# Edge words of 22 bits, lookups of the left-over maxima moved behind, and the short tile's neighbour sums with x as weights

## The reference, cut to what matters

```python
# layer 0: attention over neighbours
q = x[sub] @ Wq.T + bq ; k = x[obj] @ Wk.T + bk          # for the 10,000 pairs
scores = zeros(8, n, n).at[:, sub, obj].set((q * k).sum(-1) / 8)
scores = where(adj == 0, -inf, scores); diagonal = 1e-7
x = layernorm(x + (softmax(scores).sum(0) / 8) @ x)
# layer 1: graph convolution
x = layernorm(x + adj @ (x @ W) + bias)
```

## Time and profile before

| | |
|---|---|
| median of 3 runs | 176.11 us (175.93 to 176.72) |
| profiled execution | 176.58 us, its span 174.8 us |
| PE busy | 164.5 us, 94% |
| DVE, ACT, POOL busy | 122.4, 73.5, 71.1 us |
| mean granted TensorE clock | 0.994 |

### The profile page before, as it was taken

How to read it: one execution, slowest core, us unless ns; L and a number is a source line. 1 busy time by engine, 2 the same in 40 slices (tenths; PEclk the granted TensorE clock), 3 DMA queues, 4 the chain that set the end, 5 groups by cost and what they waited for, 6 DMA issues and landing times.

```text
span 174.8 us, 2906 instructions
## 1 busy us (share of the span) xinstructions
PE 164.5 (94%) x1054; PEld 88.1 (50%) x1054; DVE 122.4 (70%) x365; ACT 73.5 (42%) x124; POOL 71.1 (41%) x91
## 2 busy tenths in 40 slices
PE   3999999999999999979999999999999989999960
PEld 3964545565564445434445457545664434444440
DVE  2886689998978997594935866498972167657481
ACT  6867639769523333195041116142122004232441
POOL 7787777777777775248821704000000000000000
PEclk9999999999999999999999999999999999999997
DMA  5999889995299411030000530000000001311233
GB/s 133 392 368 307 323 274 363 393 387 218 77 338 325 167 60 60 4 63 0 0 1 4 159 101 6 0 2 0 4 0 0 7 6 67 117 60 73 84 120 120
DMA packets 12999, 22.65 MB, mean 130 GB/s; under 512 B 4478, under 2 KB 5662, under 8 KB 12850
## 3 DMA queue, kind: packets, MB, share of 16 engines
q1 hardware_dynamic: 7570, 18.17, 29.5%
q10 hardware_dynamic: 3280, 3.07, 5.1%
q0 software_dynamic: 2128, 1.16, 3.1%
HBM read 16.70 MB, written 5.68 MB: 128 GB/s over the span
## 4 chain that ended last, share of the span: by engine, by line
PE 90%; DVE 5%; POOL 1%; issue 1%; ACT 1%; DVEq 0%; POOLq 0%
PE acc L1250 27%; PE acc L1183 22%; PE acc L1329 12%; PE tr L1183 8%; PE tr L1169 4%; PE tr L1164 4%; PE tr L1329 3%; PE acc L1353 2%; PE tr L1287 2%; PE tr L1319 2%; PE tr L1197 1%; DVE st L832 1%; PE tr L1308 1%; PE tr L1304 1%; DVE last_st L1144 0%
## 5 line engine op out<-in xcount | busy, mean ns | idle before, releaser
L594 POOL DMA_INDIRECT ed_adj<-in_adj,ed_idx x47 | 48.5, 1032 | 14.5 <-issue 14.0
L1250 PE MATMUL acc<-adjT,x1s 128*128 128x512 f16 (+3 forms) x264 | 52.5, 354 | 0.9 <-DVE x1s L895 0.9
L1183 PE MATMUL acc<-xs,adjT 128*128 128x512 f16 (+1 forms) x176 | 40.1, 379 | 0.0
L1250 PEld LDWEIGHTS acc<-adjT,x1s 128*128 128x128 f16 (+1 forms) x264 | 24.9, 98 | 25.4 <-DVE x1s L895 1.4
L1183 PEld LDWEIGHTS acc<-xs,adjT 128*128 128x128 f16 (+1 forms) x176 | 16.8, 98 | 18.7
L1329 PE MATMUL acc<-whl,xs 128*128 128x512 f16 (+1 forms) x108 | 23.8, 370 | 0.0
L1329 PEld LDWEIGHTS acc<-whl,xs 128*128 128x128 f16 x108 | 10.6, 98 | 11.8
L1183 PE MATMUL tr<-xs,adjT 128*128 128x512 f16 (+1 forms) x66 | 15.2, 379 | 0.0
L686 ACT ACTIVATE xs<-acc 128x512 f16<-128x512 f32 (+1 forms) x12 | 6.4, 540 | 20.7 <-PE acc L1250 20.7
L638 ACT CAST adjT<-stage 128x1408 f16<-128x1408 f32 x9 | 12.3, 1361 | 3.6 <-DMA stage<-in_adj_T 3.3
L602 POOL DMA_INDIRECT found<-in_adj,top_i x8 | 10.6, 1320 | 6.3 <-DVE top_i L922 4.1
(11 more groups left out here) (250 smaller groups left out, 221.4 us busy)
## 6 DMA issues: line engine op xcount, KB each, us to landing
stage<-in_adj_T SPq DMA_DIRECT2D x9, 704.0 KB, 7.1
x_sb<-in_x SPq DMA_DIRECT2D x3, 768.0 KB, 6.3
sums_dram<-y ACTq DMA_DIRECT2D x6, 256.0 KB, 3.3
sums_dram<-xd ACTq DMA_DIRECT2D x5, 256.0 KB, 4.5
out<-y SPq DMA_DIRECT2D x5, 256.0 KB, 2.0
stage<-in_adj_T SPq DMA_DIRECT2D x3, 384.0 KB, 5.8
hot<-row_dram SPq DMA_DIRECT2D x1, 1024.0 KB, 9.8
stage<-in_L_gnn_weight SPq DMA_DIRECT2D x1, 1024.0 KB, 5.6
```

The source lines that it names most:

```text
L594: nc.gpsimd.indirect_dma_start(out=ed_adj[0:EP, c:c + 1], out_offset=None, in_=adj_flat, in_offset=bass.IndirectOffsetOnAxis(ap=ed_idx[0:E ...
L1183: last = mm(sum_bank(i)[:, :], adjT[0:width[k], k, i * P:(i + 1) * P], xs[0:width[k], half, k, :], start=(k == 0 and half == 0), stop=(k = ...
L1250: ins = mm(mix_bank(u)[:, 0:j - i], x1s[0:width[k], half, k, f * P:(f + 1) * P], adjT[0:width[k], k, i:j], start=(k == 0 and half == 0), s ...
```

## The change

1. Words: `bit_eye` becomes 65 columns wide. Two columns of a block, w and w + 64, share one 22-bit word: `fold_eye` holds 1 where row and column agree and 2^11 in the row 64 further on, and each block scales it by 2^k / 64. The words are folded as int32; the table's two halves are cut out with a mask and a shift. The diagonal's bit is no longer subtracted.
2. Candidates: the left pairs get a MAX8 of their own, directly behind the selects, and the eight gathers are for these. The looked-up pairs (exact) and the eight gathered ones are joined afterwards, in `top_candidates`, which now stands behind the splits of the weights; flags are set there, before the keys are decoded. The count of candidates is in two parts (`left_over`, `many_candidates`), and `MANY` is multiplied later, after a wait of its own.
3. The short tile leaves the loop. Blocks of `xs` are weights (128 x 128) and the 74 columns of `adjT` stream: 88 matmuls into `tr[2]`. The selects stand after its second quarter. ScalarE copies the result to `short_T`, TensorE runs six rows of the mix, and then transposes it into the tile's bank with four f32 transposes.
4. `MIX_ORDER` alternates units 0 and 1 over k, and the places of the small steps move by one to two rows. `low_x1` of tile 9 moves ahead of the candidates.
5. POOL's fill of `stackL` moves behind the gathers of the maxima.

```diff
+WP = P // 2
+WORD_ONE = 2.0 ** -6
-MIX_ORDER = [(u, k) for u in range(2) for k in range(T - 1)] + [(u, T - 1) for u in range(2)] + ...
+MIX_ORDER = [(u, k) for k in range(T - 1) for u in range(2)] + [(u, T - 1) for u in range(2)] + ...
-        bit_eye = sb("bit_eye", [P, T, P + 1], f16)
-        folded = sb("folded", [P, P], i16)
+        bit_eye = sb("bit_eye", [P, T, WP + 1], f16)
+        fold_eye = sb("fold_eye", [P, WP], f16)
+        folded = sb("folded", [P, WP], i32)
...
@@ gpsimd
-            for k in range(T):
-                nc.gpsimd.memset(power[:, k:k + 1], float(2 ** k)).then_inc(consts, 1)
+            nc.gpsimd.affine_select(out=fold_eye[:], in_=fold_eye[:], compare_op=ALU.not_equal, fill=float(2 ** T),
+                                    base=-WP, pattern=[[-1, WP]], channel_multiplier=1).then_inc(consts, 1)
...
-            pool.wait_ge(edges_looked_up, 16 * LOOKED)
-            nc.gpsimd.memset(stackL[0:64, :], 1.0).then_inc(ones_laid, 1)
             pool.wait_ge(top_ready, 1)
             for c in range(TOP):
...
+            pool.wait_ge(edges_looked_up, 16 * LOOKED)
+            pool.wait_ge(top_found, 16 * TOP)
+            nc.gpsimd.memset(stackL[0:64, :], 1.0).then_inc(ones_laid, 1)
@@ scalar
-                nc.scalar.mul(bit_eye[:, k, 0:P], ident16[:], float(2 ** k)).then_inc(bit_eye_ready, 1)
+                nc.scalar.mul(bit_eye[:, k, 0:WP], fold_eye[:], WORD_ONE * 2 ** k).then_inc(bit_eye_ready, 1)
...
+                if i == T - 1:
+                    act.wait_ge(short_done, 1)
+                    nc.scalar.copy(short_T, tr[2][:, 0:KF * LAST]).then_inc(short_copied, 1)
@@ vector, fold
-                (V.scalar_tensor_tensor(folded[:] if i == 0 else new, ident16[:], diag_bit[:, i:i + 1], bank[:, 0:P], ALU.mult, ALU.add)
+                V.tensor_scalar(folded[:] if i == 0 else new, bank[:, 0:WP], 1.0 / WORD_ONE, None, ALU.mult).then_inc(words_folded, 1)
@@ left_candidates
+                step(V.max(left_key, left_cand))
+                step(V.tensor_copy(left_i8[:, 0], left_key))
+                step(V.tensor_scalar(left_i8[:, 1], left_i8[:, 0], 11, None, ALU.logical_shift_right))
+                step(V.tensor_scalar(left_i8[:, 2], left_i8[:, 0], 2047, None, ALU.bitwise_and))
+                step(V.scalar_tensor_tensor(pos[0:EP, 0], left_i8[:, 1], float(N), left_i8[:, 2], ALU.mult, ALU.add))
+                V.tensor_scalar(ti[:, 3], pos[0:EP, 0], -1.0, 0.0, ALU.add, ALU.max).then_inc(top_ready, 1)
@@ top_candidates, now called where flag was computed
                 dve.wait_ge(edges_looked_up, 16 * LOOKED)
-                step(V.max(best, cand))
+                dve.wait_ge(top_found, 16 * TOP)
+                step(V.scalar_tensor_tensor(cand[:, LOOKED:LOOKED + TOP], got, 1.0, left_key, ALU.is_equal, ALU.mult))
+                step(V.max(best, cand[:, 0:LOOKED + TOP]))
+                V.tensor_scalar(flag[0:EP], best, 0.0, None, ALU.is_gt).then_inc(flags_ready, 1)
...
@@ behind onehot
+            many_candidates()
@@ table
-                    V.tensor_copy(table[:], folded[:]).then_inc(table_ready, 1)
+                    V.tensor_scalar(fold_in[:, 0, :], folded[:], 2 ** T - 1, None, ALU.bitwise_and).then_inc(dve_step, 1)
+                    V.tensor_scalar(fold_in[:, 1, :], folded[:], T, None, ALU.logical_shift_right).then_inc(dve_step, 1)
...
+                    V.tensor_copy(table[:], fold_in[:, :, :].rearrange("p a w -> p (a w)")).then_inc(table_ready, 1)
@@ tensor
-                    last = mm(tr[t % 2][:, 0:P + 1], adjT[:, k, t * P:(t + 1) * P], bit_eye[:, k, :], ...)
+                    last = mm(tr[t % 2][:, 0:WP + 1], adjT[:, k, t * P:(t + 1) * P], bit_eye[:, k, :], ...)
...
-            for i in range(2, T):
+            for i in range(2, T - 1):
...
+            pe.wait_ge(y_ready, T - 2)
+            for f in range(KF):
+                for k in range(T):
+                    for half in range(2):
+                        last = mm(tr[2][:, f * LAST:(f + 1) * LAST], xs[0:width[k], half, k, f * P:(f + 1) * P],
+                                  adjT[0:width[k], k, (T - 1) * P:N], start=(k == 0 and half == 0), stop=(k == T - 1 and half == 1))
+                if f == 1:
+                    for n in range(LOOKS):
+                        select(n)
+            last.then_inc(short_done, 1)
...
-            mix_rows(0, 43)
+            mix_rows(0, 6)
+            pe.wait_ge(slot_consts, 3)
+            pe.wait_ge(short_copied, 1)
+            for f in range(KF):
+                last = nc.tensor.transpose(sum_bank(T - 1)[0:LAST, f * P:(f + 1) * P], short_T[:, f * LAST:(f + 1) * LAST], ident[:])
+            last.then_inc(sums_done, 1)
+            mix_rows(6, 43)
             pe.wait_ge(flags_ready, 1)
...
-            mix_rows(43, 49)
+            mix_rows(43, 48)
             pe.wait_ge(onehot_ready, 1)
+            pe.wait_ge(many_ready, 1)
+            mm(acc[3][:, MANY:MANY + 1], ones16[0:EP, :], many16[0:EP, :], start=True, stop=True)
```

More of the change, by code:

```diff
@@ L30 @@
 LOOK_AT = (0, 3, 6, 9)
-MIX_ORDER = [(u, k) for u in range(2) for k in range(T - 1)] + [(u, T - 1) for u in range(2)] + [(u, k) for u in range(2, 12) for k in range(T)]
+MIX_ORDER = [(u, k) for k in range(T - 1) for u in range(2)] + [(u, T - 1) for u in range(2)] + [(u, k) for u in range(2, 12) for k in range(T)]
 OUT_ORDER = (*range(5), T - 1, *range(5, T - 1))
@@ L89, in resnorm_graph @@
         y = sb("y", [P, 2, H])
-        co = sb("co", [P, 8, T])
-        two_c0, neg_c0, gain, inv, eps_row, diag_bit, power, aii_all = (co[:, n, :] for n in range(8))
+        co = sb("co", [P, 6, T])
+        two_c0, neg_c0, gain, inv, eps_row, aii_all = (co[:, n, :] for n in range(6))
         st = sb("st", [P, 2, 12])
@@ L148, in resnorm_graph @@
         many = sb("many", [P, 1])
+        some = sb("some", [P, 1])
         many16 = sb("many16", [P, 1], f16)
@@ L920, in top_candidates, with many_candidates @@
                 steps += 3
-                step(V.scalar_tensor_tensor(pos[0:EP, 0], ti[:, 1], float(N), ti[:, 2], ALU.mult, ALU.add))
-                V.tensor_scalar(ti[:, 3], pos[0:EP, 0], -1.0, 0.0, ALU.add, ALU.max).then_inc(top_ready, 1)
+            def many_candidates():
+                step(V.scalar_tensor_tensor(ed_junk[0:EP, 0:LOOKED + TOP], cand[:, 0:LOOKED + TOP], 0.0, ones[0:EP, 0:LOOKED + TOP],
+                                            ALU.is_gt, ALU.mult, accum_out=some[0:EP]))
+                V.tensor_scalar(many16[0:EP], some[0:EP], many[0:EP], float(TOP), ALU.add, ALU.is_gt).then_inc(many_ready, 1)
             for i in range(T):
                 if i == T - 1:
+                    low_x1(T - 2)
                     left_candidates()
@@ L950, in _ @@
             V.memset(mix[:, :, :, N:NP], 0.0)
-            step(V.scalar_tensor_tensor(ed_junk[0:EP], cand, 0.0, ones[0:EP, 0:EC], ALU.is_gt, ALU.mult, accum_out=many[0:EP]))
-            step(V.tensor_scalar(many16[0:EP], many[0:EP], float(TOP), None, ALU.is_gt))
-            step(V.tensor_scalar(pos[0:EP, 2], best, 0.0, None, ALU.is_gt))
+            left_over()
             for n in range(2):
@@ L1168, in words @@
                 for k in ks:
-                    last = mm(tr[t % 2][:, 0:P + 1], adjT[:, k, t * P:(t + 1) * P], bit_eye[:, k, :], start=(k == 0), stop=(k == T - 1))
+                    last = mm(tr[t % 2][:, 0:WP + 1], adjT[:, k, t * P:(t + 1) * P], bit_eye[:, k, :], start=(k == 0), stop=(k == T - 1))
                 if ks[-1] == T - 1:
@@ L1232, in _ @@
                     sum_neighbours(i, range(a, b), range(2))
-                    if i == T - 1 and n == 1:
-                        for c in range(LOOKS):
-                            select(c)
+            pe.wait_ge(y_ready, T - 2)
[8 more added lines that the diff above has]
+            last.then_inc(short_done, 1)
             def mix_rows(first, last):
@@ L1273, in _ @@
             last.then_inc(xobj_T, 1)
-            mix_rows(61, 64)
+            mix_rows(60, 63)
             pe.wait_ge(xsub_in, 16)
@@ L1313, in _ @@
             last.then_inc(change_T, 1)
-            mix_rows(126, 131)
+            mix_rows(124, 129)
             pe.wait_ge(dT_lo, 1)
```

66 lines of the change are left out of this document (35 added, 31 removed).

## The result

The changed kernel takes 174.78 us in the median of 10 runs (173.54 to 176.27), against 176.19 us (175.93 to 178.42) for the kernel before on the same chip: a ratio of 0.99, 95% interval 0.9858 to 0.9941. It is 1.4 us faster in the medians, about a quarter of the forecast 5.2, and lies outside the range of 170.1 to 172.8. The ratios leave out runs in which the chip was in a slower state (here the one of 176.27), the medians do not. The profiled execution took 174.71 us with a span of 173.0, against 176.58 and 174.8.

A forecast was written before the change was run, and what follows sets the result against it. The prediction took TensorE, 94% busy, to bound the kernel. Words -3.55, short tile -1.83, transposes +0.55, stall -0.91 and new wait +0.5 gave -5.24 us: 170.9 us against 176.11, range 170.1 to 172.8.

The forecast's parts named there:

- The matmuls: TensorE's words, short tile and transposes: 3.55 us less, 1.83 us less and 0.55 us more.
- the stall on x1: TensorE's wait on DVE's low half of x1 for tile 9: would go, 0.91 us less.
- Do the others keep up before S?: Tiles before the short tile: whether DVE and ACT stay ahead of the faster TensorE; DVE 0.3 us late at tile 7.
- S: The moment tile 9's sums end on TensorE: 66.26 us before, moving to about 62.7 by the words.
- All of the 3.55 us gets through: Up to tile 9's sums: the narrower words' whole saving of 3.55 us shortens the span.
- rival 2: Tiles 5 to 9: DVE sets the pace, picks come late for looks, lag up to 0.8 us, 171.7 us; chance 0.10.
- The lookups behind: Gathers of the maxima: landing at 84.5 us, flags at 85.2, TensorE there at 85.6, so no wait at the flags.
- rival 1: Gathers of the maxima: one more slowed beside a DVE split delays flags, one-hot and count by 1.4 us, 172.3; chance 0.20.
- The new wait of 0.5 us: TensorE behind the one-hot: waits 0.5 us for DVE's key decoding and two counting ops.
- The sum: Whole kernel: -3.55 - 1.83 + 0.55 - 0.91 + 0.5 = -5.24 us.

The follow-up runs named there:

- all_fixes: Changed kernel with the edits of back_half, casts_later and cols_late together; 170.97 us, ratio 0.9697 to the kernel before.
- casts_later: Changed kernel with ScalarE's cast of tile 8 behind the root of tile 4 instead of ahead; 173.58 us, ratio 0.9885 to the kernel before.
- cols_late: Changed kernel with the broadcast of `cols` issued behind the last three loads of `adj` instead of ahead; 173.09 us, ratio 0.9818 to the kernel before.
- chunks: Changed kernel with each of the two splits of the weights cut into four pieces of 512 columns; 173.55 us, ratio 0.9829 to the kernel before.
- fill_early: Changed kernel with POOL's fill of `stackL` ahead of its wait for the gathers' addresses; 174.14 us, ratio 0.9869 to the kernel before.
- back_half: Changed kernel with fill_early and chunks, block 2's low half and the bias split behind the one-hot, count's matmul behind the compaction; 172.61 us, ratio 0.978 to before.

## Why the prediction was wrong

**The matmuls: right.** Words at 32 ns against 29.6, 3.25 us saved instead of 3.55; the short tile 2.97 against 2.92; transposes 0.44 against 0.55; the stall on x1 gone, 0.91. Their sum is 5.50 us, against 5.74 predicted.

**"Do the others keep up before S? ... All of the 3.55 us gets through": this failed.** S was forecast at about 62.7 and came at 64.34, for the 1.18 us before the look and 0.41 for casts. At tile 7, where I had DVE 0.3 us late, it took up the sums 1.9 us after their end (53.66 against 51.77; 0.2 is usual). I had taken ScalarE's casts against the moment at which TensorE wants them, and DVE's tile time against TensorE's. I had not looked at what is queued behind a cast that waits for its load. The load does not move when TensorE gets faster: the cast of tile 8 starts at 38.68, and at 38.18 in the kernel before. There, by its timeline, DVE still waited for TensorE behind this root (0.23 us before the `y` at 42.98 and 0.73 before the one at 49.02), so the late root cost nothing. It was hardly a matter of DVE's own throughput, as rival 2 had it: with the root at its place only 0.16 to 0.30 us of the 1.34 before the look is left, none in all_fixes, and S comes at 62.76 to 62.93 (62.85 in all_fixes). That is shown by casts_later, which touches only the order of ScalarE's queue, and by cols_late, which moves only a transfer. DVE's pace has this part in it: its tiles are hardly shorter than TensorE's (5.1 and 5.4 us behind the late root against 5.5 and 5.6), so that it won back only some 0.5 us of the delay by tile 7.

**"The lookups behind ... No wait there": this failed too.** Two terms of it were wrong. From addresses to landing I took 15.2 us, as before; it was 16.3 (71.05 to 87.34), since the two splits now fall wholly upon gathers, 2.87 and 3.02 us instead of 2.50 and less. This is rival 1's mechanism, with 1.1 us instead of 1.4. The other term no rival had: "POOL's fill of the ones row moves behind the gathers and before the slot indices, with 2 us to spare" counts only who waits for the fill. The fill also starts at the very moment at which the flags are computed, and holds them 0.76 us. It is the blocking that I had cited for rival 1, only with POOL ahead of DVE. Together the wait is 1.49; chunks leaves 0.32 of it, fill_early 0.74, and back_half, which has both and the reordered DVE queue, nothing.

**The new wait of 0.5 us: right in size, in part by luck.** It is 0.41 at the count. I had the flags ready 0.4 us before TensorE and 3.1 us from them to the count; in fact TensorE waited for the flags, which took that lead away, and it was 2.7 us from them to the count (88.72 to 91.43). The two errors cancel.

**The sum.** -5.50 + 1.59 (S) + 1.49 (flags) + 0.41 (count) is -2.0 us, against -1.8 in the span. Without the two terms that failed it would have been -5.50 + 0.41 = -5.1, and all_fixes, which has the change's matmuls and none of the three waits (one of 0.36 for a cast stays), takes 170.97 us. It also loses the 0.41 at the count, so that its agreement with 170.9 is within half a microsecond, not exact. Its S (62.85 against 62.7) and its arrival at the flags (85.64 against 85.6) are the forecast's steps. Two slips weigh little: S before is 66.09 by TensorE's timeline (66.26 comes from the chain, which starts a piece at the recorded end of the one before it), so that S came 1.8 us late rather than 1.6; and the lower end of the range is 170.4 - 0.16 = 170.2, not 170.1.

The chances were too sure. Rivals 1 and 2 were weighed as alternatives with 0.20 and 0.10, each with the time that it gives alone. But they sit in different stretches of the kernel, so a loss could come in both, and did, in front by another mechanism than rival 2's.

## What to carry to other kernels

When the bounding engine gets faster, list the waits of every other engine in the stretch, short ones too, and for each ask what it waits for: a wait for a transfer does not shrink, and all that is queued behind it becomes late. Two waits in different stretches add up; they are not rivals. A fill on GpSimd or a long elementwise op on VectorE is free only if nothing short of the other one of the two engines stands on the path at the same moment; put fills in known gaps, and try cutting long ops with two operands in SBUF in pieces while GpSimd issues gathers.

## What the runs showed of the hardware

A gather that starts within a two-operand DVE op of 2.3 us lasts to 0.8 us beyond that op's end (2.87 and 3.02 us instead of 0.94), and pieces of 512 columns hold it up by 0.3 us at most; it fits that GpSimd gets in between two pieces, which no run here tests by itself. I had expected that. I had not expected the reverse for tiny ops: a memset by GpSimd held DVE ops on 4 and 8 columns (1.20 us in chunks and 0.93 in the changed kernel, instead of 0.17), though not a MAX8. The Trainium skill ("SBUF — State Buffer", "Who interferes with whom") agrees: it calls the port pair that VectorE and GpSimd share an exclusive lock, says that against a VectorE op in a two-port mode whoever issues first keeps it for its whole instruction, and names `tensor_scalar` among the ops that can enter such a mode.

Gathers hold such small ops too. DVE and POOL of casts_later:
```profile
50.22 0.42 DVE L834 TENSOR_SCALAR co<-co 128x2 f32<-128x2 f32 x1
```
```profile
49.71 0.94 POOL L599 DMA_INDIRECT ed_adj<-in_adj,ed_idx  x1 [0.30 <-issue]
```
The op on two columns takes 0.17 us elsewhere and ends here with the gather, at 50.64 and 50.65; one at 49.08 takes 0.34 instead of 0.19 and ends at 49.42, with the gather before (49.41). This tile of DVE is 5.78 us long (46.46 to 52.24), and 5.44 in cols_late, where no such op is held and TensorE loses 0.16 us before the look and not 0.30. No run tests this by itself.

Narrow matmuls with a new 128x128 f16 load each stood 32 ns apart with 65 columns and 33.8 ns with 74. Only 1.8 ns lie between them, for 9 columns more.
